# Rounding through bit codes, and a split float32r convolution from block 1 on

## What is computed

```python
K = 2.0 * einsum('hn,hnl->hl', Ct, exp(P)).real          # per channel, 512 taps
y = irfft(rfft(u, n=2*L) * rfft(K, n=2*L)[None])[..., :L] # causal convolution
y = (y + u * D[:, None]) * mask                           # mask: token < length
def fq(x, w_q, in_scale, w_scale):
    x_q = clip(x / in_scale, -448, 448)
    x_dq = x_q.astype(float8_e4m3fn).astype(float32) * in_scale
    return einsum('bsh,ih->bsi', x_dq, w_q * w_scale)
hidden = silu(fq(y, gate_w, ...)) * fq(y, up_w, ...)      # 512 -> 1376
out = x + fq(hidden, down_w, ...)                         # 1376 -> 512
```

## Time and profile before

| | us |
|---|---|
| median of 3 runs | 323.29 (323.17 to 323.96) |
| span of the profiled execution | 323.2 |
| PE busy | 310.3 (96%) |
| DVE busy | 303.1 (94%) |
| ACT busy | 206.5 (64%) |
| chain that ended last | PE 77%, DVE 15%, issue 3%, DMA 3%, ACT 2% |

### The profile page before, as it was taken

How to read it: one execution, slowest core, us unless ns; L and a number is a source line. 1 busy time by engine, 2 the same in 40 slices (tenths; PEclk the granted TensorE clock), 3 DMA queues, 4 the chain that set the end, 5 groups by cost and what they waited for, 6 DMA issues and landing times.

```text
span 323.2 us, 4716 instructions
## 1 busy us (share of the span) xinstructions
PE 310.3 (96%) x1591; PEld 161.8 (50%) x1591; DVE 303.1 (94%) x460; ACT 206.5 (64%) x318; POOL 13.7 (4%) x25
## 2 busy tenths in 40 slices
PE   1979999999999999999999999999999999999996
PEld 1456655545455454555455454555545554444443
DVE  6969999999999999999989999899998999999894
ACT  4938788278765868376863958366864859545550
POOL 3031000000001000010001000010000000010010
PEclk9999999999999999999999999999999999999999
DMA  6869999500001690067401690046600770070028
GB/s 201 170 174 218 240 292 363 220 1 2 0 0 13 128 357 26 1 117 243 159 0 16 126 360 19 0 80 202 239 0 0 132 261 0 3 130 0 0 26 235
DMA packets 14015, 38.42 MB, mean 119 GB/s; under 512 B 1470, under 2 KB 6558, under 8 KB 11052
## 3 DMA queue, kind: packets, MB, share of 16 engines
q1 hardware_dynamic: 8412, 26.61, 23.9%
q0 software_dynamic: 5584, 11.57, 20.5%
HBM read 33.93 MB, written 15.81 MB: 154 GB/s over the span
## 4 chain that ended last, share of the span: by engine, by line
PE 77%; DVE 15%; issue 3%; DMA 3%; ACT 2%; DVEq 0%; SPq 0%
PE gate_ps L604 20%; PE up_ps L604 20%; PE down_ps L542 17%; PE y_ps L528 15%; DVE hv L917 3%; DVE yq L901 2%; DVE ht L925 2%; DVE yt L890 2%; DVE hq L934 2%; PE down_ps L558 2%; PE y_ps L558 1%; DMA toep<-kpad_scratch 1%; DVE ym L882 1%; PE y_ps L655 1%; DMA kpad_scratch<-hq 1%
## 5 line engine op out<-in xcount | busy, mean ns | idle before, releaser
L415 ACT ACTIVATE sil<-gate_ps,fac 128x512 f32<-128x512 f32 (+1 forms) x88 | 59.8, 681 | 71.4 <-PE gate_ps L604 70.5
L604 PE MATMUL gate_ps<-yq,wg 128*128 128x512 bf16 (+2 forms) x372 | 89.5, 363 | 0.5 <-DVE hv L917 0.3
L604 PE MATMUL up_ps<-yq,wu 128*128 128x512 bf16 (+2 forms) x372 | 89.5, 363 | 0.0
L528 PE MATMUL y_ps<-xt,toep 128*128 128x512 f32 (+1 forms) x248 | 78.1, 434 | 0.0
L917 DVE SCALAR_TENSOR_TENSOR hv<-up_ps,fac,sil 128x512 f32<-128x512 f32 (+1 forms) x88 | 65.5, 744 | 6.9 <-ACT sil L415 3.5
L542 PE MATMUL down_ps<-wd,hq 128*128 128x512 bf16 (+1 forms) x264 | 67.9, 379 | 0.0
L397 ACT ACTIVATE hc<-hv 128x1024 f32<-128x1024 f32 (+1 forms) x48 | 47.0, 980 | 17.1 <-DVE hq L934 16.7
L604 PEld LDWEIGHTS gate_ps<-yq,wg 128*128 128x128 bf16 x372 | 36.0, 100 | 41.0 <-issue 2.2
L528 PEld LDWEIGHTS y_ps<-xt,toep 128*128 128x128 f32 x248 | 45.8, 190 | 20.0 <-issue 2.4
L604 PEld LDWEIGHTS up_ps<-yq,wu 128*128 128x128 bf16 x372 | 36.3, 100 | 38.3
L925 DVE SCALAR_TENSOR_TENSOR ht<-hc,hv 128x1024 f32<-128x1024 f32 (+1 forms) x48 | 54.2, 1129 | 0.9 <-ACT hc L397 0.9
(11 more groups left out here) (163 smaller groups left out, 133.8 us busy)
## 6 DMA issues: line engine op xcount, KB each, us to landing
xt<-in_xT SPq DMA_DIRECT2D x8, 1024.0 KB, 7.8
out<-in_x SPq DMA_DIRECT2D x7, 1024.0 KB, 5.7
out<-res POOLq DMA_DIRECT2D x7, 1024.0 KB, 7.7
toep<-kpad_scratch SPq DMA_DIRECT2D x6, 1024.0 KB, 10.1
toep<-kpad_scratch SPq DMA_DIRECT2D x8, 256.0 KB, 5.1
wd<-in_down POOLq DMA_DIRECT2D x1, 1280.0 KB, 21.9
xt<-in_x SPq DMA_DIRECT2D x1, 1024.0 KB, 7.4
out<-xt SPq DMA_DIRECT2D x3, 256.0 KB, 3.2
```

The costliest lines, as they stand in the source:

```text
L415: nc.scalar.activation(sil[b][0:w, :], gate_ps[b][0:w, :], ACT.Silu, scale=fac[0:w, S_GATE:S_GATE + 1]).then_inc(silu_done, 1)
L528: last = nc.tensor.matmul(y_ps[h % 2][:, d * P:L], toep[par][:, h, d * P:(d + 1) * P], xt[par][:, h, 0:L - d * P], start=(d == 0), stop=(d ...
L604: mm = nc.tensor.matmul(ps[b][0:w, cols], wt[:, k, c * P:c * P + w], yq[par][:, version, k, cols], start=(k == 0), stop=(k == LB - 1))
```

## The change

**Rounding.** Instead of a sum and a difference in float32, values are scaled so that their bits are small; ACT reads the upper 16 bits of each float32 as an unsigned integer, multiplies by 1/16, adds 1/32 and writes a 16-bit integer (a conversion that rounds) into `yq` or `hq` (`code_y`, `code_h`). DVE multiplies by 16 and bounds it in the same 16 bits (`bound_y`, `bound_h`), and a second pass reads them as bf16, scales and bounds (`finish_y`, `finish_h`). The tiles `ym`, `yc`, `yt`, `hc`, `ht` go. Mask and scaling of y are one DVE operation per version (`scale_y`), reading PSUM.

**Convolution.** Block 0 keeps float32 and a table of its own (`kfirst_scratch`, `toep_a`), its first channel no longer in halves. From block 1 on K is split into a high part (rounded to float32r when ACT copies it, into `krow_h`) and a low part (DVE's difference, `krow_l`, by `low_k`), each with a table in DRAM and two SBUF tiles (`th`, `tl`). x is split likewise for two channels at a time: `high_x` on ACT (a copy of 128 x 1024), `low_x` on DVE (a difference). Each distance is three float32r matmuls: high x high, high taps x low x, low taps x high x. `krow_h` and `krow_l` lie in `yq[1]`.

Lines of the diff, cut:

```diff
+Y_SCALE, H_SCALE = 2.0 ** -80, 2.0 ** -20
+CODE = 2.0 ** -120
+CODES_PER_HIGH, MIDDLE_OF_HIGH = 2.0 ** -4, 2.0 ** -5
+HIGH_PER_CODE = 16.0
+LOWEST = float(0x8000 + 16 * 0x7E)
...
-        toep = [sb(f"toep{i}", [P, HB, L]) for i in range(2)]
+        toep_a = sb("toep_a", [P, HB, L])
+        th = [sb(f"th{i}", [P, HB, L], F32R) for i in range(2)]
+        tl = [sb(f"tl{i}", [P, HB, L], F32R) for i in range(2)]
+        xh = [sb(f"xh{i}", [P, 2, L], F32R) for i in range(2)]
+        xl = [sb(f"xl{i}", [P, 2, L], F32R) for i in range(2)]
...
+        krow_h = inside(yq[1], 0, C, KB)[0:KA].bitcast(F32R)
+        krow_l = inside(yq[1], C * KB, C, KB)[0:KA].bitcast(F32R)
...
@@ sync
             def load_toep(g, par):
-                sp.dma_start(toep[par][:], toep_d[g]).then_inc(conv_in[par], 16)
+                sp.dma_start(th[par][:].bitcast(F32), high_d[g]).then_inc(conv_in[par], 16)
+                sp.dma_start(tl[par][:].bitcast(F32), low_d[g]).then_inc(conv_in[par], 16)
...
+                sp.wait_ge(k_copied, 2 * b)
+                sp.dma_start(bass.AP(khigh, lo * ROW + PADK, [[KB, KA], [ROW, n], [1, KB]]),
+                             krow_h[:, lo:lo + n, :].bitcast(F32)).then_inc(k_stored[b], 16)
+                sp.wait_ge(k_split, 2 * b)
+                sp.dma_start(bass.AP(klow, lo * ROW + PADK, [[KB, KA], [ROW, n], [1, KB]]),
+                             krow_l[:, lo:lo + n, :].bitcast(F32)).then_inc(k_stored[b], 16)
...
@@ gpsimd
-            pool.wait_ge(toep_first[2 * HB - 1], 16)
+            pool.wait_ge(toep_first[2 * HB - 1], 32)
...
@@ scalar
+            def high_x(g, par, half, pair):
+                at_least(act, xt_in[par], 16 * (half + 1))
+                at_least(act, y_ready, HB * (g - 1) + 2 * pair + 2)
+                nc.scalar.copy(xh[pair][:], xt[par][:, 2 * pair:2 * pair + 2]).then_inc(x_high, 1)
+            def code_y(g, par, h):
...
+                at_least(act, yv_done, m + 1)
+                at_least(act, up_ready, CH * (g - 1))
+                values = high(yv[h % 2][:]).rearrange("p v (k b) -> p (v k) b", k=LB)
+                nc.scalar.activation(yq_of(par, h).bitcast(U16), values, ACT.Copy, bias=MIDDLE_OF_HIGH,
+                                     scale=CODES_PER_HIGH).then_inc(y_coded, 1)
...
+            for i, stored_k in enumerate(k_stored):
+                act.wait_ge(stored_k, 32 if i else 16)
+            slots(0, 0, 0, True, 2)
...
@@ tensor, conv
-                    at_least(pe, ym_done, m - 1)
+                        at_least(pe, conv_in[par], 32 * half)
+                    at_least(pe, x_split, 2 * (g - 1) + h // 2 + 1)
+                    at_least(pe, yv_done, m - 1)
                 for d in distances:
-                    last = nc.tensor.matmul(y_ps[h % 2][:, d * P:L], toep[par][:, h, d * P:(d + 1) * P],
-                                            xt[par][:, h, 0:L - d * P], start=(d == 0), stop=(d == 2))
+                    for n, (taps, xs) in enumerate(((th, xh), (th, xl), (tl, xh))):
+                        last = nc.tensor.matmul(y_ps[h % 2][:, d * P:L], taps[par][:, h, d * P:(d + 1) * P],
+                                                xs[h // 2][:, h % 2, 0:L - d * P], start=(d == 0 and n == 0),
+                                                stop=(d == 2 and n == 2))
...
@@ vector
+            def low_k(i):
+                for half in range(2):
+                    dve.wait_ge(k_copied, 2 * (i - 1) + half + 1)
+                    v.tensor_tensor(rows_of_k(i, half, krow_l), k_in_bank(i, half),
+                                    rows_of_k(i, half, krow_h).bitcast(F32), ALU.subtract).then_inc(k_split, 1)
+            def low_x(g, pair):
+                at_least(dve, x_high, 2 * (g - 1) + pair + 1)
+                v.tensor_tensor(xl[pair][:], xt[g % 2][:, 2 * pair:2 * pair + 2], xh[pair][:].bitcast(F32),
+                                ALU.subtract).then_inc(x_split, 1)
+            def scale_y(g, h):
...
+                v.scalar_tensor_tensor(yv[q][:, 0, :], y_ps[q][:], f(D_GATE), masked, ALU.mult, ALU.mult)
+                v.scalar_tensor_tensor(yv[q][:, 1, :], y_ps[q][:], f(D_UP), masked, ALU.mult,
+                                       ALU.mult).then_inc(yv_done, 1)
+            def bound_y(g, par, h):
...
+                v.tensor_scalar(codes, codes, HIGH_PER_CODE, LOWEST, ALU.mult, ALU.min).then_inc(y_bounded, 1)
+            def finish_y(g, par, h):
...
+                v.tensor_scalar(yq_of(par, h), yq_of(par, h), Y_SCALE / CODE, TOP * Y_SCALE, ALU.mult,
+                                ALU.min).then_inc(yq_ready, 1)
...
+SCALE_PLAN = {0: 1, 3: 2, 5: 3}
+CODE_PLAN = {0: 0, 1: 1, 4: 2, 6: 3}
+FINISH_PLAN = {1: 0, 2: 1, 5: 2, 7: 3}
+HIGH_PLAN = {4: 0, 8: 1}
+LOW_PLAN = {5: 0, 9: 1}
```

More of the change, by code:

```diff
@@ L425, in slots @@
-                    if ahead and c in MAGNITUDE_PLAN and not (first and MAGNITUDE_PLAN[c][1] == 0):
-                        magnitude_y(g + 1, MAGNITUDE_PLAN[c][1])
-                    if ahead and c in SCALE_PLAN and not (first and SCALE_PLAN[c][1] == 0):
-                        scale_y(g + 1, SCALE_PLAN[c][1])
+                        code_h(g - 1, 1 - par, PAIRS - 1, n - 1)
+                    if c and c % 2 == 0:
+                        code_h(g, par, c // 2 - 1, n)
+                    if ahead and c in CODE_PLAN:
+                        code_y(g + 1, 1 - par, CODE_PLAN[c])
@@ L444, in _ @@
-                magnitude_y(0, h)
+                code_y(0, 0, h)
+                if h < 2:
+                    act.wait_ge(xt_in[1], 16)
+                    nc.scalar.copy(xh[h][:], xt[1][:, 2 * h:2 * h + 2]).then_inc(x_high, 1)
             copy_k(2)
-            scale_y(1, 0)
-            magnitude_y(1, 0)
-            slots(0, 0, None, True, 2)
+            for i, stored_k in enumerate(k_stored):
+                act.wait_ge(stored_k, 32 if i else 16)
+            slots(0, 0, 0, True, 2)
@@ L514, in _, with conv_first @@
             warm(WARM[3])
+            def conv_first(h):
+                pe.wait_ge(toep_first[h], 16)
+                if h == 0:
+                    pe.wait_ge(xt_in[0], 16)
+                at_least(pe, yv_done, h - 1)
+                for d in (0, 1, 3, 2):
+                    last = nc.tensor.matmul(y_ps[h % 2][:, d * P:L], toep_a[:, h, d * P:(d + 1) * P],
+                                            xt[0][:, h, 0:L - d * P], start=(d == 0), stop=(d == 2))
+                last.then_inc(y_ready, 1)
             def conv(g, par, half, h, distances):
@@ L991, in slots @@
-                    if first and c == 1:
-                        round_y(1, 1, 0)
-                        clip_y(1, 1, 0)
-                    elif ahead and c in MASK_PLAN:
-                        mask_y(g + 1, MASK_PLAN[c])
-                    if c < 3 and not first:
-                        left_over(g, par, c, before, behind)
-                    if c in plan and c < 9 and not (first and c == 3):
-                        rounded(PAIRS * g + plan[c], g, par, plan[c])
-                    if ahead and c in SUM_PLAN and not (first and c == 2):
-                        sum_y(g + 1, SUM_PLAN[c])
@@ L1067, in _ @@
-            rounded_sum(last, PAIRS - 1)
-            clip(last - 1, 1, PAIRS - 2)
-            rounded(last, NBLK - 1, 1, PAIRS - 1)
-            clip(last, 1, PAIRS - 1)
+                    if c == 1 and not first:
+                        bound_h(PAIRS * g - 1, 1 - par, PAIRS - 1)
+                        finish_h(PAIRS * g - 1, 1 - par, PAIRS - 1)
+                    if ahead and c in SCALE_PLAN:
+                        scale_y(g + 1, SCALE_PLAN[c])
+                    if c and c % 2 == 0:
+                        bound_h(m - 1, par, c // 2 - 1)
@@ new lines, in slots @@
+                    if ahead and c in FINISH_PLAN:
+                        bound_y(g + 1, 1 - par, FINISH_PLAN[c])
+                    if c and c % 2 == 0:
+                        finish_h(m - 1, par, c // 2 - 1)
+                    if ahead and c in FINISH_PLAN:
+                        finish_y(g + 1, 1 - par, FINISH_PLAN[c])
+                    if ahead == 2 and c in LOW_PLAN:
+                        low_x(g + 2, LOW_PLAN[c])
+                    if c == CH - 1 and ahead == 2:
+                        scale_y(g + 2, 0)
@@ new lines, in _ @@
+            low_k(1)
+            scale_y(0, 0)
+            scale_y(0, 1)
+            bound_y(0, 0, 0)
+            finish_y(0, 0, 0)
+            low_x(1, 0)
+            scale_y(0, 2)
+            bound_y(0, 0, 1)
+            finish_y(0, 0, 1)
+            scale_y(0, 3)
+            bound_y(0, 0, 2)
+            finish_y(0, 0, 2)
+            bound_y(0, 0, 3)
+            finish_y(0, 0, 3)
+            low_x(1, 1)
+            scale_y(1, 0)
+            low_k(2)
+            dve.wait_ge(k_ready, 2 * len(K_GROUPS))
@@ L1071, in _ @@
+            slots(0, 0, 2, True)
+            for g in range(1, NBLK - 2):
+                slots(g, g % 2, 2, False)
+            slots(NBLK - 2, 0, 1, False)
```

(4 more changed lines are left out.)

326 lines of the change are left out of this document (80 added, 246 removed).

## The result

The changed kernel takes 333.38 us (median of 4 runs, 330.44 to 335.69) against 323.23 for the kernel before on the same chip: a ratio of 1.0281, 95% interval 1.0227 to 1.0335. It is slower, by 10 us by the medians and 9 by the ratio; the forecast was 321.1. Its four runs spread over 5 us, the longer two (335.0 and 335.69) at a mean granted clock of 0.983 and 0.982 and the shorter two (331.77 and 330.44) at 0.990 and 0.988, and the longest is left out of the ratio.

A forecast was written before the change was run, and what follows sets the result against it. The prediction took PE, running back to back, as the bound, with DVE close behind. From 323.2: -0.3 tail, -11.2 convolution, +5.2 start, +1.0 clock, +3.2 slot 7 gave 321.1 us; range 309 to 333, likeliest case 315 to 325.

The forecast's parts named there:

- PE is the bound, rounding worth nothing: Blocks: PE runs back to back, so the new rounding on DVE and ACT lies beside it and alone gains nothing.
- Convolution, -11.2: Blocks 1 to 7: three float32r matmuls at bf16's pace, 1.72 us a channel, saving 0.43 over 26 channels: -11.2 us.
- Shows 50 ns, twice a channel: Convolution: a weight load behind a 128-column matmul is not fully hidden, adding 0.10 us a channel.
- two rivals on float32r: Convolution: short matmuls spaced by 190 ns loads (334.6 us, chance 0.12), or 512 columns taking 0.43 us (about 357, 0.10).
- The start, +5.2: Before slots(0): ACT waits for the klow store, landing after 6.5 us, moving PE's third gate group to 44.3: +5.2 us.
- its upper end, +8: Start: the klow store also queues behind eight table loads instead of four, costing up to +8 us.
- Second table: [...] Nothing: First 60 us: 3 MB more to load delays the down weights, first needed after 65 us, so it costs nothing.
- The clock, +1.0: Start: after PE's pause of some 5 us its clock may fall to half, costing 0 to 2.5 us, taken as +1.0.
- Slot 7, +3.2: Blocks 4 to 7: PE stalls 0.7 to 0.8 us each in slot 7 for split x and the second table: +3.2 us.
- the 0.3 I took off: Tail: PE's 0.32 us wait for DVE goes with the new rounding: -0.3 us.
- (c): Convolution rival: float32r weight loads do not overlap short matmuls, spaced 190 ns, 2.36 us a channel: 334.6 us, chance 0.12.
- (b): Slot 7 rival: four blocks stall 2.3 us instead of 0.8 because x or second table lands late: 327 us, chance 0.13.

The follow-up runs named there:

- experiment 12: Changed kernel with its new rounding but the float32 convolution of before, K rows moved to the table tile, ACT's store wait gone: 322.30 us (0.9974).
- experiment 3: Changed kernel with the K rows in th[0] instead of yq[1] and ACT's wait for the later stores gone: 333.04 us (1.0282).
- experiment 6: Changed kernel with x loaded first and K rows in th[0], plus 34 filler matmuls during PE's 7.4 us wait in slots(0): 323.40 us (1.0003).
- experiment 1: Changed kernel with the loads of x and tables issued ahead of SP's wait for the add and the copy: 327.77 us (1.0132).
- Experiments 1 and 2: experiment 1, and the changed kernel with only the first high_x moved from slot 4 to slot 5 in ACT's queue: 327.68 us (1.0147).

## Why the prediction was wrong, point by point

**PE is the bound, rounding worth nothing.** Right. DVE lost 14.5 us a block and the block stayed at 37.15 (experiment 12). In the changed kernel a block has 23.11 us of DVE and 20.89 of ACT, forecast 25 and 23.

**Convolution, -11.2.** The direction was right, the term too large. "So a channel costs 3 x 1280 x 0.216/512 + 0.10 = 1.72 us": it costs 1.88, so 0.27 is saved and not 0.43, 7 us over 26 channels. The step that failed is bf16's pace for the longer matmuls: 512 columns are 0.232 apart and not 0.216, and over the nine longer matmuls of a channel the excess is 0.13 us. "Shows 50 ns, twice a channel" was nearly right: behind three matmuls of 128 columns in a row the next one starts 0.06, 0.11 and 0.12 us later, 0.13 more than their columns at bf16's pace, against the 0.10. Of the two rivals on float32r neither came: the starts are not 0.19 apart whatever the columns, nor 0.43 for 512. The rule I cited, that the fast weight load is off for FP32 ("TensorE: Matmul & The Clock Gate", weight-path perf modes, in the Trainium skill), fits float32r by its load of 190 ns against bf16's 99.

**The start, +5.2.** The mechanism was right, ACT waits for `klow`, and the size short: +6.7 (45.75 for 39.06). The store was issued at 34.92, a little earlier than I reckoned, and landed 8.6 us later instead of 6.5. I had its upper end, +8, with this very reason. I did not ask what is late next, and experiment 3 shows that it mattered: even with this wait gone the tables of block 2 hold PE until 58. "Second table: [...] Nothing" was the wrong step there, and came out in the changed kernel only because the longer wait covered it. I costed the megabytes against the down weights alone.

**The clock, +1.0.** The mechanism was right and the size short: one drop costs 1.5 us in experiment 6, and at the start of the changed kernel PE worked 3.1 us at 0.50, which is as much. In the profile of experiment 1 it was 5.6 us. There were two drops, the second after a wait of 2 us in slots(5). I had the mechanism for one pause only.

**Slot 7, +3.2.** Wrong in place. "ACT, in slot 4, stands before high_x from about 16.5: behind it in its queue are the SiLUs, and DVE waits for those." I followed this queue towards DVE and the split, and found PE just late in slot 7. The same queue holds `down_scaled` of slot 5, and PE waits for that bank at once, two slots earlier. In slot 7 PE never waited in these blocks: in slots(3) x was split at 167.8, the matmul came at 169.0. The four blocks were the right ones; the price was 5.0 us of waits and one drop of the clock, 7.3 us by the block starts. Experiments 1 and 2 each take the waits away, for 5.6 us by the medians. The wait for DVE's low part that I forecast exists, 1.0 us, but at the first convolution of block 2, for which I had no term.

**Sum.** From the block starts: +8.4 to slots(1); then six blocks that win 6.4 (undisturbed, 213.3 us in experiment 1, for 219.75) and lose 7.3; +0.7 from the start of slots(7) to the end: +10.0. The forecast had -2.1. Of the 12 us between, about 4 are the convolution, 3 the start (1.5 the wait for the store, 1.0 the wait for the low part of x, 0.5 the clock), 4 the waits in slot 5 against the 3.2 I had, with the clock behind them, and the rest the tail. There the 0.3 I took off did come: from the start of slots(7) to DVE's last operation it is 38.3 us for 38.9. But the last stores land later (the last one 2.7 us after its issue for 1.7), and the gain was lost; why they do is open. The range, up to 333, missed the median by 0.4. The sign rival that came closest in number, (c) with 334.6, was right by accident, since its mechanism is absent; (b), slower by a late x, had the right culprit at the wrong place.

## What to carry to other kernels

When an instruction that waits for a DMA is added to an engine, list everything behind it in that engine's queue until the landing, drains of PSUM banks above all, and price the first one that the bounding engine needs. Then either load earlier or put the waiting instruction behind those: one small edit did it either way here, for about 5 us. And when a wait at the start is removed, compute the landing of the next transfer before counting the gain: with the DMA engines full, what helps is to send first the bytes that are read first.
